# Histogram of a graph layer: the lower-key rows of the first forty pairs made on ScalarE from TensorE products, statistics of x moved within the order

## What is computed

```python
xn = _layernorm(x, axis=-1)                  # statistics over the 256 features of a node
ef = edge_emb[edge_type_ids]                 # 4 edge types
esum = jax.ops.segment_sum(ef, src, num_segments=N)
cnt = jax.ops.segment_sum(jnp.ones((ef.shape[0], 1), ef.dtype), src, num_segments=N)
x = x + esum / jnp.maximum(cnt, 1.0)
q = (x @ Wq + bq).reshape(N, H, C)           # and k, v, and the skip projection
```

## Time and profile before

| what | value |
|---|---|
| median of 3 runs | 2830.92 us (2825.3 to 2831.41) |
| the profiled execution: its own time | 2825.32 us |
| its span | 2823.6 us |
| granted TensorE clock, mean of the span | 0.955 |
| first pair's one-hots start | 21.79 us |
| last pair's counts leave PSUM | 248.09 us |

### The profile page before, as it was taken

One profiled execution on the slowest core, in us unless ns is written; L12 is line 12 of the kernel. 1 busy time (PEld: TensorE's weight loads), 2 busy tenths in 40 slices (PEclk: granted clock), 3 DMA queues, 4 the chain that ended last, 5 costly groups with the idle time before them and its releaser, 6 DMA issues.

```text
span 2823.6 us, 50437 instructions
## 1 busy us (share of the span) xinstructions
PE 2508.7 (89%) x15651; PEld 2177.1 (77%) x15651; DVE 2236.2 (79%) x4398; ACT 1532.6 (54%) x3157; POOL 939.5 (33%) x891
## 2 busy tenths in 40 slices
PE   4388996899898898998998998759999999999999
PEld 2266774677777777777776776549999999999998
DVE  8797554899999999999999999756677777666775
ACT  0411110465665656655665656556666666666665
POOL 0330003666666666666666666300000000000000
PEclk9699998899999999999999999869999999999999
DMA  5210445766666666666666666510000000000000
GB/s 166 79 46 21 147 137 186 214 201 202 199 196 204 195 200 205 193 198 201 200 198 195 204 202 196 153 43 16 11 11 15 15 15 15 15 15 11 11 14 10
DMA packets 189958, 335.56 MB, mean 119 GB/s; under 512 B 31456, under 2 KB 129008, under 8 KB 189766
## 3 DMA queue, kind: packets, MB, share of 16 engines
q0 software_dynamic: 67104, 219.09, 25.9%
q1 hardware_dynamic: 116378, 108.11, 12.6%
q10 hardware_dynamic: 6316, 6.40, 0.8%
HBM read 293.81 MB, written 40.48 MB: 118 GB/s over the span
## 4 chain that ended last, share of the span: by engine, by line
PE 55%; DVE 18%; issue 6%; ACT 2%; DVEq 1%; DMA 1%; ACTq 0%; SPq 0%
PE ps L1324 16%; PE ps L1221 9%; PE ps L1210 8%; PE ps L1334 8%; PE ps L1188 4%; DVE ring L1658 3%; PE ps L1181 3%; DVE ring L1711 2%; PE ps L1166 2%; ACT f_more L953 1%; DVE f_split L1842 1%; DVE nodes L1725 1%; PE ps L1306 1%; DMA relq<-rel_rows 1%; DVE f_more L1858 1%
## 5 line engine op out<-in xcount | busy, mean ns | idle before, releaser
L777 POOL DMA_INDIRECT ring<-kv_rows,idx x832 | 887.4, 1067 | 738.9 <-DMA idx<-src_cols 294.8
L1324 PE MATMUL ps<-f_split,e_up 128*128 128x256 f32 (+1 forms) x3200 | 595.6, 286 | 3.5 <-DVEq L1872 1.3
L953 ACT ACTIVATE f_more<-ps,e_rest 128x256 f32<-128x256 f32 (+1 forms) x800 | 402.2, 553 | 277.7 <-PE ps L1324 276.6
L1324 PEld LDWEIGHTS ps<-f_split,e_up 128*128 128x128 f32 x3200 | 498.3, 192 | 17.4 <-issue 8.0
L1210 PE MATMUL ps<-nodes,ohT 128*128 x1664 | 413.8, 393 | 63.2 <-DVE ring L1658 56.9
L1842 DVE TENSOR_TENSOR f_split<-f_more,f_split 128x512 fp32r<-128x512 f32 (+1 forms) x400 | 272.8, 682 | 229.0 <-ACT f_split L958 222.1
L1324 PE MATMUL ps<-f_split,e_low 128*128 128x256 f32 (+1 forms) x1600 | 453.0, 283 | 0.0
L1221 PE MATMUL ps<-ring 128*128 128x260 f32 x1664 | 447.3, 415 | 0.0
L1210 PEld LDWEIGHTS ps<-nodes,ohT 128*128 128x128 f32 x1664 | 319.8, 196 | 133.0 <-issue 86.9
L1221 PEld LDWEIGHTS ps<-ring 128*128 128x128 f32 x1664 | 317.7, 201 | 43.6
L885 ACT ACTIVATE nodes<-ps 128x780 f32 x208 | 170.9, 822 | 270.3 <-PE ps L1221 249.8
(11 more groups left out here) (314 smaller groups left out, 3556.2 us busy)
## 6 DMA issues: line engine op xcount, KB each, us to landing
relq<-rel_rows SPq DMA_DIRECT2D x208, 128.0 KB, 4.2
ring<-kv_rows,idx POOLq DMA_INDIRECT x832, 4.3
kv_rows<-work SPq DMA_DIRECT2D x49, 256.0 KB, 2.0
xn_rows<-nodes SPq DMA_DIRECT2D x1, 6272.0 KB, 20.4
sx_rows<-work SPq DMA_DIRECT2D x49, 128.0 KB, 1.8
nodes<-in_x_dram ACTq DMA_DIRECT2D x4, 1536.0 KB
work<-in_x_dram SPq DMA_DIRECT2D x48, 128.0 KB, 2.1
m_xn<-xn_rows SPq DMA_DIRECT2D x24, 256.0 KB, 4.3
```

Of the source, the lines that this page charges most:

```text
L777: pool.indirect_dma_start(out=kvh(c)[:, g, 0:2 * D], out_offset=None, in_=kvD, in_offset=bass.IndirectOffsetOnAxis(ap=idx[c // KP][:, s:s ...
L953: ins = act.activation(f_whole[l][:, m * T2 * P:m * T2 * P + n * P], bank(2 * l + e % 2, m * T2 * P, m * T2 * P + n * P), ACT.Relu, bias=e ...
L1324: last = pe.matmul(bank(2 * l + e % 2, m * T2 * P, m * T2 * P + n * P), e_parts[l][w][:, e, i, m * P:(m + 1) * P], src_[a][:, i * T2 * P:i ...
```

## The change

For the first 40 pairs the lower one-hots are no longer made by DVE. A product on PE (`steps_of`) spreads, for 4 columns at a time, the lower keys minus a threshold over 4x128 places of a PSUM bank (bank 6 or 7, half a pair each); the first of every 16 pairs starts from the thresholds (`fall`), the others add the difference to the pair before (`swap`). ACT takes the sign of it into the half of `loh` (L810 of the changed kernel). PE tallies rows of plus and minus ones into places 0 to 195 of bank 4, the other 58 pairs into places 256 to 451. At the end one product (`unstep`) turns the sums of signs into counts and adds them.

The constants become HA, HB, HI1, HI3 = 5, 12, 17, 20, and a new one HX = 25: the slot keys come after 34 pairs, the statistics of x after 40, the tables of slots after 50. The gram moves to the last 48 pairs, one or two to each. All loops around pairs are written out.

```diff
-    HA, HB, HI1, HI3 = 4, 9, 13, 15
-    GT, GG = 8, 6
-    GI = (NW - 1) // GG
+    HA, HB, HI1, HI3, HX = 5, 12, 17, 20, 25
...
+            act.wait_ge(sem("ident"), 2)
+            act.activation(pick, ident[:, :], ACT.Copy).then_inc(sem("steps_in"), 1)
+            act.wait_ge(sem("hist_keys"), 1)
+            act.activation(lo_rows, lo_f, ACT.Copy).then_inc(sem("steps_in"), 1)
+            for c in range(2 * HI3):
+                act.wait_ge(sem("hist_ps"), reuse(c, 2))
+                if c == 0:
+                    act.wait_ge(sem("early_ps"), 3)
+                for h in range(2):
+                    act.wait_ge(sem("steps_ps"), 2 * c + h + 1)
+                    act.activation(loh[c % 2][:, h * 512:(h + 1) * 512], bank(6 + h), ACT.Sign).then_inc(sem("steps_made"), 1)
+
...
+            act.wait_ge(sem("hist_ps"), done(2 * HI3 - 1))
+            act.activation(stepped, bank(4, 0, NK), ACT.Copy).then_inc(sem("ends_sb"), 1)
...
+            def steps_of(c):
+
+                lo = lo_rows[:, c // 16 * P:(c // 16 + 1) * P]
+                for h in range(2):
+                    q = c % 16 * G + h * G // 2
+                    if c:
+                        pe.wait_ge(sem("steps_made"), 2 * c - 1 + h)
+                    if c % 16 == 0:
+                        pe.matmul(bank(6 + h), ones_b, fall.unsqueeze(1).broadcast_to([1, G // 2, P]), start=True, stop=False, skip_group_check=True)
+                    which = swap if c % 16 else pick
+                    pe.matmul(bank(6 + h), lo, which[:, q:q + G // 2].unsqueeze(2).broadcast_to([P, G // 2, P]), start=False, stop=False,
+                              skip_group_check=True).then_inc(sem("steps_ps"), 1)
...
+            pe.wait_ge(sem("steps_in"), 4)
+            steps_of(0)
+            for c in range(2 * HI1):
+                steps_of(c + 1)
+                tally(c, c % 2)
...
+            pe.wait_ge(sem("ends_sb"), 3)
+            pe.matmul(bank(4, 256, 256 + NK), unstep, stepped, start=False, stop=False, skip_group_check=True)
+            t = 0
+            for c in range(2 * HX, 2 * HI):
                 tally(c, c % 2)
+                while t * (2 * HI - 2 * HX) < (c + 1 - 2 * HX) * NW:
+                    gram(t, t % 2)
+                    t += 1
...
                 for o, k, n in ((loh[b], loC, P), (koh[b], keyC, NK)):
+                    if o is loh[b] and c < 2 * HI3:
+                        continue
...
+            histogram(HI3, HX - HI3)
             dve.wait_ge(sem("rows_in"), 32 * NB)
...
-            histogram(HI3, HI - HI3)
+            histogram(HX, HI - HX)
```

More of the change, by code:

```diff
@@ L77, in gps_layer_kernel @@
     HI = HT // (2 * G)
[L78 to L81 removed]
+    HA, HB, HI1, HI3, HX = 5, 12, 17, 20, 25
+    assert HI1 < HI3 < HX < HI and G == 8
     CREDIT = 2
+    ORDER_GAPS, ORDER_FLAG, SLOT_KEYS, SLOT_COLS, SLOT_ROW, X_VAR, X_SHIFT, GRAM_ZERO = range(1, 9)
     def done(g):
@@ L283, in gps_layer_kernel @@
         pads_i = work[0:1, 6600:7112].bitcast(I32)
+        lo_rows = work[:, 4100:4100 + NSP // 2].bitcast(BF16)
+        pick = work[:, 4548:4612].bitcast(BF16)
+        swap = work[:, 4612:4676].bitcast(BF16)
+        fall = work[0:1, 4676:4740].bitcast(BF16)
+        ones_b = work[0:1, 4740:4804].bitcast(BF16)
+        unstep = work[:, 4804:4804 + P]
+        stepped = work[:, 2860:2860 + NK]
+        assert NSP == 896 and 2860 + NK <= 4100
         relB = slot(10)[:, 0:NSP // 2].bitcast(BF16)
@@ L1014, in gram @@
                 last.then_inc(sem("gram_ps"), 1)
[L1015 to L1019, removed]
+            pe.wait_ge(sem("steps_in"), 4)
[3 more added lines that the diff above has]
+                tally(c, c % 2)
+            pe.wait_ge(sem("prep_made"), SLOT_KEYS)
             for b in range(NB):
@@ L1025, in _ @@
             last.then_inc(sem("early_ps"), 1)
-            for c in range(2 * HI1, 2 * HI3):
+            for c in range(2 * HI1, 2 * HX):
+                if c + 1 < 2 * HI3:
+                    steps_of(c + 1)
                 tally(c, c % 2)
             pe.wait_ge(sem("tables_made"), 1)
-            pe.wait_ge(sem("slots_made"), 3)
+            pe.wait_ge(sem("prep_made"), SLOT_ROW)
             turn(relR, 0).then_inc(sem("early_ps"), 1)
@@ L1036, in _ @@
             last.then_inc(sem("early_ps"), 1)
-            pe.wait_ge(sem("gram0"), 1)
+            pe.wait_ge(sem("prep_made"), GRAM_ZERO)
             for i in range(2):
                 pe.matmul(bank(6 + i, 0, D + 1), zero_g[:, 0:P], zero_g, start=True, stop=False, skip_group_check=True)
[L1040 to L1047, removed]
+            pe.wait_ge(sem("ends_sb"), 3)
+            pe.matmul(bank(4, 256, 256 + NK), unstep, stepped, start=False, stop=False, skip_group_check=True)
+            t = 0
+            for c in range(2 * HX, 2 * HI):
                 tally(c, c % 2)
+                while t * (2 * HI - 2 * HX) < (c + 1 - 2 * HX) * NW:
+                    gram(t, t % 2)
+                    t += 1
             pe.wait_ge(sem("marks_made"), 1)
@@ L1415, in histogram @@
             def histogram(first, n):
-                with dve.Fori(0, n) as it:
-                    for b in range(2):
-                        one_hot_keys(it * 2 + (first * 2 + b), b)
+                for c in range(first * 2, (first + n) * 2):
+                    one_hot_keys(c, c % 2)
             histogram(0, HA)
```

49 lines of the change are left out of this document (30 added, 19 removed).

## The result

| what | before | after |
|---|---|---|
| median of 9 runs each | 2831.41 us | 2840.39 us (2832.11 to 2842.81) |
| the profiled execution: its own time | 2825.32 us | 2840.08 us |
| its span | 2823.6 us | 2838.4 us |
| granted TensorE clock, mean of the span | 0.955 | 0.958 |
| the first pair's tally starts | 23.43 us | 44.53 us |

The ratio is 1.0028, with a 95% interval of 1.0017 to 1.0038: slower by 9.0 us in the medians. The last counts came 8.75 us later. The profiled execution of before was its fastest. What lies behind the last counts took 2575.5 us of the span in it and 2581.6 in the changed kernel's (2568.7 to 2582.3 in experiments 1 to 6), so I follow the last counts in the traces and the ratio in the times.

The account below looks back on a forecast made before the run. DVE was taken to set the pace at 1.49 us a pair. Slot columns +8.7, restart -6.2 and last pairs +2.9 gave +5.4 us: 2830.7 for the profiled execution, 2836 for the median, range 2824 to 2848.

Parts of the forecast that it names:

- Step 1: First tally: starts later because ACT's Signs wait until ACT has issued the loads of x; +19.7 us.
- Step 2: First forty pairs: a loop between PE and ACT gives 1.26 us a pair against 1.49; -9.2 us.
- Step 3: Order check, slot keys and their sums: 14.8 us; slot columns at 106.0 us, net +8.7 with start and pace inside.
- Step 4: Statistics 23.7 us, ten pairs 14.9, tables 13.9; the pairs hide gathers and most of the normalising; further cost nothing.
- Step 5: Restart behind the tables: DVE waits 5.5 us (3.9, then 1.6 more) against 11.7; -6.2 us.
- Step 6: Slow stretch of pairs beside POOL's work: moves along, its loss of 12.7 us stays; net 0.
- Step 7: Last 48 pairs: grams make PE the bound at 1.57 to 1.58 us a pair over DVE's 1.49; +2.9 us.
- A: First forty pairs: longer loop between ACT and PE, at pace 1.49 the 9.2 gain is gone; +14.6, 2845.5 us; 15%.
- C: First forty pairs: no loop, ACT and PE interleave at 1.15 us; +1, 2832 us, no change; 10%.
- B: First forty pairs: PE at its lower clock (0.50), 2.3 us a pair; +41, 2872 us; 5%.
- D: Slow stretch is due to the store of x, not POOL, and nearly vanishes; 11 us less, 2824 us; 17%.

Follow-up runs that it names:

- experiments 1 to 6: Five variants of the changed kernel and one of the kernel before, altering who loads x, the signs, the spreads or the tables' place; medians 2817.10 to 2840.86 us.
- Kernel 1: Changed kernel with the five loads of x issued by SP instead of ACT; 2818.71 us, ratio 0.9956 to the kernel before.
- Kernel 4: Changed kernel with spreads made two pairs ahead in four banks, the tally between the halves; 2831.53 us, ratio 1.0000 to the kernel before.
- chain_tables_late: Changed kernel with POOL's tables of chains held back until the histogram is done, store of x unmoved; single run, 2859.15 us.
- Kernel 6: Changed kernel with the tables of slots after 40 pairs instead of 50 (HX = 20); 2840.86 us, ratio 1.0032 to the kernel before.
- before_loads_on_sp: Kernel before the change, with the five loads of x issued by SP; 2835.11 us, ratio 1.0008 to the kernel before.
- no_signs: Changed kernel with its new order but all lower one-hots made by DVE, no spreads, Signs or unstep product; 2821.67 us, ratio 0.9966 to the kernel before.

## Why the prediction was right or wrong, step by step

The forecast was 2836, the result 2840.4. By the last counts the forecast was +5.4, measured +8.75. The ratio, 1.0028, lies just outside the 0.2% that the forecast had itself just inside; of the three outcomes "slower" (0.43) came, by the path described. The steps were right in kind; one term, the time to the slot columns, was 5.3 us too small, and smaller errors behind it hid a part of that.

**Step 1, the start, right in kind.** Forecast +19.7, measured +21.1 at the first tally: 0.7 because the load of x ended at 38.70 and not 38.02; 0.4 because the second spread of pair 1, which waits for pair 0's second Sign, stands ahead of that tally (it starts at 44.13, the tally at 44.53) and the forecast had left it out; the rest in the first products and signs. Kernel 1 shows the cause.

**Step 2, the pace, right:** 2.53 us for two pairs against 2.52. Kernel 4 shows that the loop sets it. Two things were missing. I priced only the first spreads at the low clock, but the first two tallies too took 1.51 (4.14 us from first to third tally, not 2.52: +1.6); and I left out that the thresholds come again at pairs 16 and 32, some 0.7 us each.

**Step 3, what lies between, right:** the order check cost 0.96 (57.66 to 59.88 from tally to tally, less 1.26); the slot keys 13.45 (90.49 to 105.20, less 1.26); with 0.5 for a slow tally behind them 14.9 against 14.8. Yet the step's end, the slot columns, was forecast at 106.0 and came at 111.27: +14.0 net instead of +8.7. Of these 5.3 us, 1.4 are the start, 1.6 the slow first pairs, 1.4 the thresholds; some 0.9 lie elsewhere, 0.4 of it because DVE was 0.6 us ahead of PE and not 1.0. This is the term that was mis-sized.

**Step 4:** statistics 23.6, ten pairs 15.1, as forecast; tables 12.8 instead of 13.9, as DVE waited less in them: -1.1. The restart came at 162.74 (forecast 158.5).

**Step 5, the restart, right, and the gain larger:** one wait of 3.45 instead of 5.5. The first part (forecast 3.9) is near; the second (1.6, for the split of the weights and the first grams) did not reach DVE, which POOL slowed down just then. In chain_tables_late, without POOL's work, both parts are there, 3.31 and 1.93. Kernel 6 confirms what removed the old wait.

**Step 6, right:** the slow stretch moved with POOL. It cost 86.08 - 46 x 1.575 = 13.6 us, against 12.7 forecast. Kernel 7 shows POOL as its cause, which the prediction could only hold likely. What the Trainium skill (GPSIMD Engine Reference, Specifications) says of the shared SBUF interfaces fits it; the run shows the effect and not the interface.

**Step 7, right:** 1.575 to 1.58 us a pair, PE busy 99% in the last 51 us.

**The balance.** +14.0 at the slot columns, -1.1 for the tables, and -8.3 at the restart (3.45 against 11.7) make +4.6; the rest of the 8.75, 4.1, is PE's pace (+2.9), the longer slow stretch (+0.9) and 0.3 in small pieces. Against the forecast, the +5.3 at the slot columns was partly cancelled by -1.1 and by the restart's -2.1: that the sum missed by only 3.35 us is in part luck. Behind the last counts a further 1.5 us went until the first projection (L1127 at 271.47, L1087 at 261.26 before). The granted clock was 0.61 in 257 to 271 us against 0.81 in the like window of before, and four products of 512 columns there (L1116, L1076 before) took 3.78 us instead of 2.31, which is the whole 1.5. before_loads_on_sp, with the old order and no signs, shows the same 3.78, and no_signs 2.36; so it is not the signs as such, and why the clock was low is not known.

**The rivals.** A (pace 1.49) and C (1.15) did not come; C's pace needed kernel 4's edit. B came for two pairs only, and for one behind the slot keys; its sum was wrong, as +41 stood on top of the forecast's +5.4 and would have given 2877, not 2872. D fell with kernel 7. A faster kernel than before was within reach, by an edit that was not in the change. The page that I weighed in step 2 (the Trainium skill, ScalarE: Activation LUTs) would have had the signs lose 16 us; with ACT free in time, they gained 7.9 at the last counts (kernels 1 and 3), since DVE works beside ACT.

## What to carry to other kernels

When work is moved to an engine that was idle, look first at what its queue issues ahead of that work: a load that nobody waits for until later held ACT for 28.8 us here, and SP, which had nothing to send in that time, could issue it at no loss. That has to be checked: in the kernel before, where SP was wanted a little sooner, the same edit cost a wait of 3.9 us. Work out two engines that hand a tile back and forth as a loop over as many tiles as there are buffers; the sum of busy times of either is only the floor. And when two gains are to be added and don't add up, compare all four kernels mark by mark before blaming a delay that looks new: with the spreads ahead, the order check and the thresholds cost the same whoever loads x, and what differed was PE's rate in its first products.

## What the runs showed of the hardware

- **Issuing a large load holds the issuing engine.** ACT did nothing else while it issued the five loads of x (6.4 MB in rows of 1 KB): 24.20 and 4.64 us; SP took 21.31 and 4.39 for the same. Whether the issuing is slow in itself or held back by the transfer is not tested. The Trainium skill (DMA: Bandwidth & Descriptors, Issuing engines are not separate DMA queues) says that issuing from several engines at once saves only the sequencer's time, which is usually small beside the transfer; here that time was worth 21.7 us.
- **A moving operand that repeats one value 128 times is as fast as a plain one:** in spreads_ahead two spreads of 512 columns stand between 49.29 and the tally at 49.72, so 0.22 us each, where products on plain operands start 0.23 apart. The prediction had held open that they would be slower (rival A).
- **The clock column can miss a slow stretch.** In the changed kernel it shows 1.00 from 41 to 48 us, while the products of 512 columns stand 0.54 us apart and the tallies last 1.51. The trace holds no record of the clock before 48.5 us there, and without a record the column says 1.00. In loads_on_sp the same durations (0.54 and 1.51) stand beside a granted clock of 0.50, and chain_tables_late, whose first forty pairs are those of the changed kernel, has 0.50 recorded from 20.0 to 47.3 us. The durations are the safer sign.
- **POOL's tables on one partition slow DVE on 128.** One-hots of 1024 and 1568 columns: 9 in 10 us with POOL busy 9.29 of them, 11 in the same 10 us with POOL's tables held back (and PE, no longer DVE, setting the pace). One of 1024 columns took 1442 ns instead of 693, one of 1568 columns 1294 instead of 970.
